# Window attention scores in three 32-row tiles on three PSUM banks, with masks as extra products, new orders and a written-out finish

## What is computed

```python
y = roll(layernorm(x), (-4, -4))                       # channels last
q, k, v = qkv(windows of 8 x 8 of y)                   # 6 heads of 16
attn = softmax(q * 16 ** -0.5 @ k.T + mask[window])    # 64 x 64 a head
x = x + roll(proj(attn @ v), (4, 4))
x = x + w2(gelu(w1(layernorm(x)) + b1)) + b2
x = x * rsqrt(gamma_eff @ (x * x) + beta_eff)          # over channels
```

## Time and profile before

| | us |
|---|---|
| median of three runs | 1937.88 (1937.69 to 1939.20) |
| profiled execution, own time | 1939.82 |
| span of the profile | 1937.9 |

### The profile page before, as it was taken

How to read it: one execution, slowest core, us unless ns; L and a number is a source line. 1 busy time by engine, 2 the same in 40 slices (tenths; PEclk the granted TensorE clock), 3 DMA queues, 4 the chain that set the end, 5 groups by cost and what they waited for, 6 DMA issues and landing times.

```text
span 1937.9 us, 70164 instructions
## 1 busy us (share of the span) xinstructions
PE 1878.0 (97%) x26628; PEld 1355.8 (70%) x26628; DVE 1610.0 (83%) x4516; ACT 1638.5 (85%) x2945; POOL 1645.4 (85%) x1801
## 2 busy tenths in 40 slices
PE   5999999999999999999999999999999999999995
PEld 3677777777777777777777777777777777777773
DVE  5888888888888888888888888888888888888873
ACT  2788888888888888888888888888888888888884
POOL 4688888888888888888888888888888888888884
PEclk9999999999999999999999999999999999999997
DMA  3122222122122122122122122122122122122110
GB/s 62 28 42 50 35 51 50 35 51 50 35 51 50 34 52 50 33 53 50 32 54 50 32 53 50 32 53 49 34 53 44 38 52 49 35 51 50 26 31 25
DMA packets 217315, 85.00 MB, mean 44 GB/s; under 512 B 117287, under 2 KB 215913, under 8 KB 216985
## 3 DMA queue, kind: packets, MB, share of 16 engines
q1 hardware_dynamic: 216262, 80.22, 21.4%
q0 software_dynamic: 128, 0.20, 0.1%
q10 hardware_dynamic: 594, 0.12, 0.0%
HBM read 28.03 MB, written 25.17 MB: 27 GB/s over the span
## 4 chain that ended last, share of the span: by engine, by line
PE 95%; DVE 2%; issue 1%; DMA 1%; ACT 1%; SPq 1%; POOL 0%; POOLq 0%; DVEq 0%
PE mm_bank L900 49%; PE score_banks L956 11%; PE probs_t_bank L967 8%; PE pv_bank L981 6%; PE turn_bank L893 6%; PE mm_bank L991 6%; PE mm_bank L934 5%; PE turn_bank L886 4%; SPq L351 0%; DVE y_tok L750 0%; DMA k_block<-k 0%; DVE row_max L779 0%; DMA x_ext<-in_x 0%; DVE shifted L787 0%; DVE x L808 0%
## 5 line engine op out<-in xcount | busy, mean ns | idle before, releaser
L438 POOL TENSOR_TENSOR hidden_lo<-hidden,hidden_hi 128x512 fp32r<-128x512 f32 x382 | 484.6, 1282 | 0.2 <-POOL hidden_hi L433 0.2
L779 DVE TENSOR_REDUCE row_max<-score_banks 128x12 f32<-128x768 f32 x256 | 243.5, 951 | 152.7 <-PE score_banks L956 152.6
L520 ACT ACT_TABLE_LOAD x256 | 328.4, 1283 | 4.5
L750 DVE TENSOR_SCALAR y_tok<-turn_bank,moments,rstd 128x96 f32<-128x96 f32 x1024 | 304.8, 371 | 10.0 <-ACT rstd L531 5.6
L587 ACT ACTIVATE hidden<-mm_bank 128x512 f32<-128x512 f32 x381 | 228.0, 598 | 76.2 <-PE mm_bank L900 60.7
L560 ACT ACTIVATE probs<-shifted 128x768 f32<-128x768 f32 x256 | 216.2, 845 | 65.8 <-DVE shifted L787 65.5
L967 PEld LDWEIGHTS probs_t_bank<-ident_sb,probs 128*128 128x128 f32 x1536 | 200.0, 141 | 82.4 <-issue 2.4
L967 PE MATMUL probs_t_bank<-ident_sb,probs 128*128 128x128 f32 x1536 | 252.2, 272 | 1.4 <-ACT probs_t L566 1.4
L566 ACT ACTIVATE probs_t<-probs_t_bank 128x384 f32<-128x384 f32 x512 | 246.1, 481 | 7.6 <-PE probs_t_bank L967 7.6
L787 DVE TENSOR_TENSOR shifted<-score_banks,row_max 128x768 f32<-128x768 f32 x256 | 245.2, 958 | 8.8
L438 POOL TENSOR_TENSOR y_lo<-y,y_hi 96x512 fp32r<-96x512 f32 x128 | 218.8, 1709 | 23.8 <-POOL y_hi L433 23.3
(11 more groups left out here) (132 smaller groups left out, 4524.3 us busy)
## 6 DMA issues: line engine op xcount, KB each, us to landing
x_ext<-in_x SPq DMA_DIRECT2D x128, 192.0 KB, 3.3
k_block<-k SPq DMA_DIRECT2D x768, 32.0 KB, 2.1
out<-o_ext SPq DMA_DIRECT2D x128, 192.0 KB, 2.8
mask_stage<-in_qmask SPq DMA_DIRECT2D x64, 32.0 KB
y_hi<-mask_stage SPq DMA_DIRECT2D x64, 32.0 KB
k_block<-in_kmask POOLq DMA_DIRECT2D x2, 96.0 KB, 5.3
w_raw<-in_w_t SPq DMA_DIRECT2D x1, 144.0 KB
w<-in_w_t SPq DMA_DIRECT2D x1, 144.0 KB
```

The lines of the kernel that those rows point to most:

```text
L438: nc.gpsimd.tensor_tensor(lo, whole, hi, ALU.subtract).then_inc(is_split, 1)
L520: nc.scalar.preload_act_table_set(name)
L750: made = nc.vector.tensor_scalar(y_tok[ln][:, c, :], turn_banks[ln][:, n * DIM:(n + 1) * DIM], moments[ln][:, c, 0:1], rstd[ln][:, c:c + 1 ...
L779: nc.vector.tensor_reduce(row_max[:, g, :, :], group_scores(), op=ALU.max, axis=AX.X)\
```

## The change

`ROW_TILES` goes from 2 to 3: q, k and their products use 32 rows for two heads, on PSUM banks 0 to 2 of `score_banks`. `scores` runs once a round, over all four window pairs: 24 products of 32 rows, 64 output rows and 128 columns (48 instructions). `max_scores`, `shift_scores` and the exponential run three times, over 512 columns of one bank. `turn_probs` transposes four window pairs of one head pair back into the same score bank, three times a round, and `probs_t_copy` empties 512 columns each time. The next half's `scores` wait until all three copies are done (`probs_t_ready`). `probs_t_bank` is gone.

The mask rows leave q, k and y1, and with them `stage_mask` and `place_mask`. Where a window is masked, `scores` adds a product of four rows (`q_quadrants` by `k_masks`) for each row tile. `round_attended` (the high part of attended) moves from POOL to VectorE; POOL keeps the difference. `MM_ITEMS` and the orders of all engines change. The rounds end at the last half's attention, and what is left is written out with `late`. In that finish the last halves' `project`, `mlp_down` and `denominators` take whole fp32 operands in one product in place of parts (`last_project`, `last_mlp_down`, `last_denominators`), and the last half's gelu writes into the space of `probs_t`. The tile widths change with it in `copy_keys`, `fold_qkv` and `set_rows`; the loads of `wproj` are one DMA instead of six.

```diff
-ROW_TILES = 2
+ROW_TILES = 3
 TILE_HEADS = HEADS // ROW_TILES
 TILE_DIM = TILE_HEADS * HEAD_DIM
-GROUPS = 2
-GROUP_PAIRS = PAIRS // GROUPS
-GROUP = GROUP_PAIRS * HEADS * TOKENS
+GROUPS = HEAD_PAIRS
 CHUNKS = HALF // 128
...
         MM_ITEMS = [
-            ("v", ATTEND, v_ready, 1, 1), ("sum", ATTEND - 1, log_sum_made, 1, 1),
-            ("den", DIVIDE, log_den_made, 1, 1), ("k", QK, k_ready, 1, 1),
-            ("mlp2", SETTLE, x3_ready, 1, 1), ("q", QK, q_ready, 1, 1), ("proj", PROJECT, x2_ready, 1, 1),
-            *((f"mlp1_{n}", MLP, gelu_ready, HID_CHUNKS, n + 1) for n in range(HID_CHUNKS)),
+            ("k", QK, k_ready, 1, 1),
+            ("sum", ATTEND - 1, log_sum_made, 1, 1),
+            ("v", ATTEND, v_ready, 1, 1),
+            ("den", DIVIDE, log_den_made, 1, 1),
+            ("q", QK, q_ready, 1, 1),
+            ("mlp2", SETTLE, x3_ready, 1, 1),
+            ("proj", PROJECT, x2_ready, 1, 1),
+            ("mlp1_0", MLP, gelu_ready, HID_CHUNKS, 1),
+            ("mlp1_1", MLP, gelu_ready, HID_CHUNKS, 2),
+            ("mlp1_2", MLP, gelu_ready, HID_CHUNKS, 3),
         ]
-        MM_AT = {item[0]: at for at, item in enumerate(MM_ITEMS)}
-        def mm_bank(name, a):
-            h = a - MM_ITEMS[MM_AT[name]][1]
-            return mm_banks[(MM_AT[name] + len(MM_ITEMS) * h) % 2]
...
+        def up_bank(A, n):
+            if A < FINAL:
+                return mm_bank(f"mlp1_{n}", A)[:, :]
+            return score_banks[:, n, :]
+        def hidden_of(A):
+            return hidden if A < FINAL else probs_t[:, (A - 1) % 2, :, :, :].rearrange("k m p t -> k m (p t)")
+        def squares_of(A):
+            return x3_sq[:, :] if A < FINAL else y1[:, 0, 0:HALF]
...
+            def rest_of_attended(A, a):
+                split_lo(attended_hi[0:DIM, :], attended_lo[0:DIM, :], attended[0:DIM, :],
+                         attended_hi_ready, attended_split, A + 1)
...
                 run(split_hidden, SETTLE)
+                run(wrap_x, TURN_IN)
+                run(rest_of_attended, PROJECT)
                 run(wrap_out, DIVIDE - 1)
-                run(wrap_x, TURN_IN)
-                run(split_attended, PROJECT)
-                run(split_y1, TURN_OUT)
-                run(split_squares, SETTLE)
+                run(round_y1, TURN_OUT)
+                run(rest_of_y1, TURN_OUT)
+                run(square, SETTLE)
+                run(round_squares, SETTLE)
+                run(rest_of_squares, SETTLE)
...
+            def probs_t_copy(A, a, g):
+                act.wait_ge(probs_turned, GROUPS * A + g + 1)
+                nc.scalar.activation(probs_t[:, a % 2, g, :, :],
+                                     score_banks[:, g, :].rearrange("k (p t) -> k p t", p=PAIRS),
+                                     ACT.Copy).then_inc(probs_t_ready, 1)
...
                 run(load_tables, MLP - 1, "natural_log_exp_and_others")
+                run(k_copy, QK)
                 run(rstd_of, TURN_OUT, 0)
                 run(rstd_of, MLP, 1)
                 run(softmax_exp, ATTEND, 0)
                 run(log_sums, ATTEND - 1)
+                run(softmax_exp, ATTEND, 1)
                 run(inverse_sums, PROJECT)
+                run(y_copy, TURN_OUT, 0)
                 run(log_denominators, DIVIDE)
-                run(k_copy, QK)
                 run(probs_t_copy, ATTEND, 0)
-                run(y_copy, TURN_OUT, 0)
+                run(q_copy, QK)
                 run(y_copy, MLP, 1)
                 run(inverse_denominators, DIVIDE)
-                run(softmax_exp, ATTEND, 1)
+                run(softmax_exp, ATTEND, 2)
                 run(probs_t_copy, ATTEND, 1)
-                run(q_copy, QK)
                 run(load_tables, MLP, "gelu_and_others")
                 run(gelu, MLP, 0)
                 run(probs_t_copy, ATTEND, 2)
                 run(gelu, MLP, 1)
                 run(gelu, MLP, 2)
-                run(probs_t_copy, ATTEND, 3)
...
+            def last_squares(A, a):
+                wait_alone(dve, x3_ready, A + 1)
+                wait_alone(dve, sq_split, FINAL - 1)
+                whole = half_of(x3, a)
+                nc.vector.tensor_tensor(squares_of(A)[0:DIM, :], whole, whole, ALU.mult).then_inc(sq_ready, 1)
...
-            def group_scores():
-                return score_banks[:, :, 0:GROUP // ROW_TILES].rearrange("t r (i k) -> t r i k", k=TOKENS)
+            def group_scores(g):
+                return score_banks[:, g, :].rearrange("t (i k) -> t i k", k=TOKENS)
             def max_scores(A, a, g):
-                dve.wait_ge(scores_made, GROUPS * A + g + 1)
-                nc.vector.tensor_reduce(row_max[:, g, :, :], group_scores(), op=ALU.max, axis=AX.X)\
+                dve.wait_ge(scores_made, A + 1)
+                nc.vector.tensor_reduce(row_max[:, g, :], group_scores(g), op=ALU.max, axis=AX.X)\
                     .then_inc(max_ready, 1)
             def shift_scores(A, a, g):
                 group = GROUPS * A + g
                 dve.wait_ge(max_ready, group + 1)
-                wait(dve, probs_ready, group - 1)
-                nc.vector.tensor_tensor(shifted[:, g, :, :, :].rearrange("t i r k -> t r i k"), group_scores(),
-                                        row_max[:, g, :, :].unsqueeze(3)
-                                        .broadcast_to([128, ROW_TILES, GROUP_PAIRS * TILE_HEADS, TOKENS]),
+                wait(dve, probs_ready, group + 1 - GROUPS)
+                nc.vector.tensor_tensor(shifted[:, g, :, :], group_scores(g),
+                                        row_max[:, g, :].unsqueeze(2)
+                                        .broadcast_to([128, PAIRS * TILE_HEADS, TOKENS]),
                                         ALU.subtract).then_inc(scores_shifted, 1)
...
+            def round_attended(A, a):
+                dve.wait_ge(attended_ready, A + 1)
+                nc.vector.tensor_copy(attended_hi[0:DIM, :], attended[0:DIM, :]).then_inc(attended_hi_ready, 1)
...
                 run(max_scores, ATTEND, 0)
+                run(max_scores, ATTEND, 1)
                 run(shift_scores, ATTEND, 0)
+                run(shift_scores, ATTEND, 1)
+                run(normalise, TURN_OUT, 0)
                 run(v_blocks, ATTEND)
-                run(normalise, TURN_OUT, 0)
                 run(normalise, MLP, 1)
                 run(divide, PROJECT)
-                run(max_scores, ATTEND, 1)
-                run(shift_scores, ATTEND, 1)
+                run(round_attended, PROJECT)
+                run(max_scores, ATTEND, 2)
+                run(shift_scores, ATTEND, 2)
                 run(split_y2, MLP)
-                if H == HALVES - 1 - SETTLE:
-                    split_last_hidden()
                 run(second_residual, SETTLE)
-                if H == HALVES - 1 - SETTLE:
-                    split_last_squares()
+                run(first_residual, PROJECT)
                 run(outputs, DIVIDE)
-                run(first_residual, PROJECT)
                 run(statistics, TURN_IN, 0)
...
+            late(normalise, FINAL - 1, 1)
+            late(divide, FINAL)
+            late(split_y2, FINAL - 1)
+            late(first_residual, FINAL)
+            late(second_residual, FINAL - 2)
+            late(statistics, FINAL, 1)
+            late(outputs, FINAL - 3)
+            late(normalise, FINAL, 1)
+            late(split_y2, FINAL)
+            late(second_residual, FINAL - 1)
+            late(last_squares, FINAL - 1)
+            late(outputs, FINAL - 2)
+            late(second_residual, FINAL)
+            late(last_squares, FINAL)
+            late(outputs, FINAL - 1)
+            late(outputs, FINAL)
...
+            def mask_kind(A, w):
+                in_last_row, is_last = (A // 2) % ROWS == ROWS - 1, w == WINDOWS - 1
+                return (2 if is_last else 1) if in_last_row else (0 if is_last else None)
+            def scores(A, a):
+                if has(A - 1):
+                    wait_alone(pe, probs_t_ready, GROUPS * A)
+                wait_alone(pe, q_ready, A + 1)
+                wait_alone(pe, keys_copied[a % 2], 16 * HEADS * (A // 2 + 1))
+                if A == 0:
                     wait_alone(pe, weights_folded, 4)
-                if has(GROUPS * A + g - 1, GROUPS * HALVES):
-                    wait_alone(pe, scores_shifted, GROUPS * A + g)
-                if g == 0:
-                    wait_alone(pe, q_ready, A + 1)
-                    wait_alone(pe, keys_copied[a % 2], 16 * HEADS * (A // 2 + 1))
+                if A == 1:
+                    wait_alone(pe, masks_loaded, 16 * MASK_CONSTS)
                 width = TILE_HEADS * TOKENS
-                for p in range(GROUP_PAIRS):
-                    for r in range(ROW_TILES):
-                        for n in range(2):
-                            w = (a % 2) * HALF_WINDOWS + 2 * (GROUP_PAIRS * g + p) + n
-                            rows = slice(64 * r, 64 * r + 64)
-                            made = nc.tensor.matmul(
```

(91 more changed lines are left out.)

304 lines of the change are left out of this document (139 added, 165 removed).

## The result

The changed kernel's median is 1863.84 us (four runs, 1861.74 to 1864.61), beside 1938.54 for the kernel before on the same chip: a ratio of 0.9612, 95% interval 0.9595 to 0.9628. The forecast was 1864.0. The profiled execution took 1864.61 us for a span of 1862.8.

The account below looks back on a forecast made before the run. TensorE, busy 97% of the span, was taken as the bound. From 1937.9 us, 79.3 off for rounds, 19.6 added for masks and 13.5 off for the finish gave 1864.7, forecast 1864; forecast case 1845 to 1884, likely range 1840 to 1925.

Parts of the forecast that it names:

- Scores: TensorE's score products each round: 1.00 us with six tiles at once, in place of 1.62, saving 0.62.
- the right choice of three: Score tiles running at once on TensorE: six (1.00 us), four (1.43 us) or two (2.71 us); six taken.
- Masks: Added mask products on the path: 0.21 us per odd half, 0.85 per last-row half, 19.6 us in all.
- The loop: Circle from scores through VectorE, POOL and TensorE to the next scores: 13.80 us counted, 13.85 taken, 0.65 less than before.
- both chains meet at `project`: VectorE and POOL's chain reaches `project` at 9.65 us, TensorE's work ahead of it at 9.60: within 0.05.
- The first rival: Longer VectorE loop: cast beside POOL takes 0.80 us, handovers add up; rounds 14.0 to 14.3, span 1884 to 1925; chance 0.21.
- Its sign: What would show the longer VectorE loop: `project` waiting on POOL's `attended_lo`.
- The hole at `project`: TensorE's 0.20 us wait for `second_residual` each round goes, as bank order lets `project` follow `project_q`, not `mlp_down`.
- The rounds' total: 122 full rounds x 0.65 us gives 79.3 us less; masks give 19.6 us back.
- the filling rounds: The first rounds, in which the stages still fill; the start was left as it is, within 1 us.
- The finish: From the last round's scores to the end: 60.5 us to near 47, saving 13.5.
- my lower bound of 8: Least saving expected in the finish, in us; the upper bound was 18.

## Why the prediction was right, and where not

- **Scores**: 1.05 us measured for 1.00 counted. Six tiles at once was the right choice of three; the order of the list proved to be its condition (14.80 a round without it). By estimate from the Trainium skill's figure for packing, "TensorE: Matmul & The Clock Gate", section on the measured speedup, it would have been near 1.4: this case's traces disagree with that.
- **Masks**: 17 to 18 us for 19.6 counted: 0.19 for an odd half's masked window (0.21 counted), 0.89 for a last row's eight (0.85). Right in kind and size.
- **The loop**: each handover came within 0.15 us of its place, the round at 13.87 for 13.85. That both chains meet at `project` was right: with the cast on POOL the difference ends 0.38 us later, and a round costs 0.30 more. The first rival (the cast beside POOL, 0.80) did not come: `attended_hi` took 0.42 in all of its 127 but one, as POOL was idle then. That one (1788.82, beside `hidden_lo` on POOL from 1788.06 to 1789.34) took 0.80, so the price was right. Its sign, `project` waiting on `attended_lo`, came only while the first rounds filled.
- **The hole at `project`**: gone as counted, but the working gave it to the bank order alone. The runs on the kernel before show that step to be wrong as a term by itself: it costs 1.14 us a round on its own, and with ScalarE's and VectorE's orders mended it gives 0.06. The other 0.14 stands there as the wait for the one bank of turned probabilities. The prediction came out right here because the change brings all of this together; it didn't see that the term needs it.
- **The rounds' total** was 8 us better than counted. I multiplied 122 rounds by 0.65 and took all the rest of the 1937.9 as fixed; in that rest were 9.6 us of long rounds, which vanished, and the masks were some 1.5 us cheaper. The first three rounds gave 3.3 of it back. A step was missing: what makes those rounds long, and whether that stays. It still isn't known. And the filling rounds were taken as unchanged: in the third, TensorE waits 1.84 us for POOL's `attended_lo`, where it waited 0.67 before.
- **The finish** gave 7.0 instead of 13.5: the term was mis-sized, because I carried the rounds' durations over to a list written out by hand and didn't look whether it also carried the rounds' table loads. With the set loaded by name the finish takes 47.8 us for the 47 counted. No run took its other parts (the whole fp32 products, the new order) one by one. At 7.0 it was also under my lower bound of 8.

The two last errors, 8.0 and 6.5 us, go opposite ways and nearly cancel. The median is right by the loop's working, and to the microsecond only by luck.

## What to carry to other kernels

Count a new round as the meeting of two or more chains, each step from a row of the old trace: here that gave the round to 0.02 us. A move on one engine's list is not an edit by itself: whoever empties the bank, and whoever reads the result, has to move too, so try the orders together. Where steady rounds are written out into a list, go through what each round does besides its work, table loads first, and look at what the long rounds of the old trace are before calling them fixed.

## What the runs showed of the hardware

- Side-by-side tiles of TensorE need their products next to each other in the list: 48 instructions over six tiles of 32 rows by 64 columns hold the engine for 1.05 us in turn over six tiles, and for 2.02 us in turn over two. In the second order a new row tile begins 0.50 us after the old one, while 6 of the old one's 16 instructions have still to start, so there are four tiles at once for part of the time, and never six.
- Without the set named, ScalarE loaded a table (1.28 us each, eight of them) at every change between a logarithm and an exponent in the finish, though one set serves both; with it named once, one load was left.
- TensorE's clock fell to half within a stretch in which it was busy throughout, behind 2.8 us of products that were mostly two tiles wide and alternately 32 and 4 rows deep (0.98, then 0.50). It did so too in an odd round, behind 2.65 us of two-wide scores and one window's masks (1.00, then 0.50 for 3.41 us).
